# A gated linear-scan mixer with a routed expert: new written-out orders per batch, four staging slots, planes added in pairs before their transposes

## The reference

```python
x = L0_attn_x                                    # (8, 1024, 256) float32
z = layernorm(x)
logits = z @ gate_W                              # 4 mixers, the best 2 are kept, softmax over the 2
g, v, d = (z @ W[m] + b[m] for W in (Wg, Wv, Wd))  # for each mixer m of 4
a = 0.001 + 0.998 * sigmoid(d)
h_t = a_t * h_(t-1) + sigmoid(g_t) * tanh(v_t)   # a scan over the 1024 tokens, per mixer
x = x + layernorm(sum over m of comb[m] * h[m])
u = layernorm(layernorm(x)) ...                  # then per batch: mean over tokens -> batchnorm -> router
e = argmax(softmax(...)); y = relu(u @ W_down[e] + b) @ W_up[e] + b
x = x + layernorm(y * gate)
```

## Time and profile before

| | us |
|---|---|
| median of 3 runs | 859.58 |
| the profiled execution | 857.58 |
| its span | 855.8 |
| batch 0, up to its T0 | 99.8 |
| batches 1 to 6, each (619.9 / 6) | 103.3 |
| batch 7 from T0, and the end | 136.1 |

### The profile page before, as it was taken

How to read it: one execution, slowest core, us unless ns; L and a number is a source line. 1 busy time by engine, 2 the same in 40 slices (tenths; PEclk the granted TensorE clock), 3 DMA queues, 4 the chain that set the end, 5 groups by cost and what they waited for, 6 DMA issues and landing times. The chain is left out here.

```text
span 855.8 us, 11078 instructions
## 1 busy us (share of the span) xinstructions
PE 686.4 (80%) x3577; PEld 364.6 (43%) x3577; DVE 601.7 (70%) x1233; ACT 464.1 (54%) x803; POOL 74.8 (9%) x57
## 2 busy tenths in 40 slices
PE   4989795798948898689987889687895878998823
PEld 2454443345423463344634336243453435543521
DVE  6878766675854949459494686846768467778886
ACT  4756254655555544755457564565645745585522
POOL 1010011001110103001030010200111001000110
PEclk9989997899978999689997999988997899999965
DMA  9700230004300061000510007000160002300003
GB/s 220 250 26 1 86 112 1 10 1 133 115 0 11 0 199 52 0 10 1 198 50 1 10 4 243 4 0 10 33 215 2 9 1 75 123 1 9 2 0 107
DMA packets 40624, 49.78 MB, mean 58 GB/s; under 512 B 6470, under 2 KB 36458, under 8 KB 40554
## 3 DMA queue, kind: packets, MB, share of 16 engines
q1 hardware_dynamic: 33164, 41.62, 15.5%
q10 hardware_dynamic: 7392, 7.34, 3.0%
HBM read 38.85 MB, written 8.52 MB: 55 GB/s over the span
## 5 line engine op out<-in xcount | busy, mean ns | idle before, releaser
L1135 PE MATMUL ps_main<-xh,w_hi 128*128 128x512 f16 x768 | 301.8, 393 | 6.5 <-ACT decay_s L494 3.9
L1135 PE MATMUL ps_main<-xh,w_lo 128*128 128x512 f16 x768 | 300.3, 391 | 0.0
L1135 PE MATMUL ps_main<-xl,w_hi 128*128 128x512 f16 x768 | 298.8, 389 | 0.0
L761 DVE TENSOR_TENSOR_SCAN hid<-decay_s,value_s 128x1024 f32<-128x1024 f32 (+1 forms) x64 | 138.1, 2158 | 6.1 <-DVE value_s L779 0.6
L494 ACT ACTIVATE gate_s<-ps_main,vecs 128x512 f32<-128x512 f32 x128 | 87.6, 685 | 99.0 <-PE ps_main L1135 92.5
L494 ACT ACTIVATE value_s<-ps_main,vecs 128x512 f32<-128x512 f32 x128 | 88.1, 689 | 94.1 <-PE ps_main L1135 92.8
L494 ACT ACTIVATE decay_s<-ps_main,vecs 128x512 f32<-128x512 f32 x128 | 88.4, 691 | 84.8 <-PE ps_main L1135 81.2
L1135 PEld LDWEIGHTS ps_main<-xh,w_hi 128*128 128x128 f16 x768 | 77.9, 101 | 98.6 <-issue 10.1
L1135 PEld LDWEIGHTS ps_main<-xl,w_hi 128*128 128x128 f16 x768 | 77.1, 100 | 97.3 <-issue 11.7
L1135 PEld LDWEIGHTS ps_main<-xh,w_lo 128*128 128x128 f16 x768 | 77.2, 100 | 87.4 <-issue 9.1
L779 DVE TENSOR_TENSOR value_s<-gate_s,value_s 128x1024 f32<-128x1024 f32 (+1 forms) x72 | 79.4, 1103 | 41.8 <-ACT value_s L494 41.6
(11 more groups left out here) (138 smaller groups left out, 587.8 us busy)
## 6 DMA issues: line engine op xcount, KB each, us to landing
comb_all<-comb_dram SPq DMA_DIRECT2D x32, 512.0 KB, 5.1
resid<-in_L_attn_x SPq DMA_DIRECT2D x8, 1024.0 KB, 5.5
x_in<-in_L_attn_x ACTq DMA_DIRECT2D x14, 512.0 KB, 7.0
out<-resid SPq DMA_DIRECT2D x7, 1024.0 KB, 8.6
expert<-experts SPq DMA_DIRECT2D x8, 192.5 KB, 2.2
x_in<-in_L_attn_x SPq DMA_DIRECT2D x2, 512.0 KB, 4.8
w_stage<-in_L_attn_Wg SPq DMA_DIRECT2D x4, 256.0 KB, 5.6
w_stage<-in_L_attn_Wd SPq DMA_DIRECT2D x4, 256.0 KB, 7.0
```

Of the source, the lines that this page charges most:

```text
L761: dve.tensor_tensor_scan(states(pc), staged(decay_s, pc, pc.c), staged(value_s, pc, pc.c), start, ALU.mult, ALU.add).then_inc(scanned, 1)
L1135: ins = pe.matmul(ps_main[:, i % BANKS], w[:, 3 * m + kind, k, half * P:(half + 1) * P], v[:, bt.par, k, chunk(c)], start=(n == 0), stop=( ...
```

## The change

- `run` is split: `run_first`, `run` and `last` each have an order of their own on every engine.
- Gates and decays have four slots (`SLOTS`), and the value of a piece goes straight to its place in `hid`; `value_s` is gone. `multiply` and `scan` work in place there. The new waits are on ScalarE, before a value is written over a plane of the batch before.
- Planes 2, 3, 6 and 7 (`SUMMED`) are weighted, and then the plane two places before (same half, the mixer before) is added on VectorE. Only these four are transposed: 32 transposes in a batch instead of 64.
- x is held once instead of twice. Its load is issued by SyncE, at the start of `run`, behind the store of the batch before; it was issued by ScalarE.
- VectorE's order: `a_moments` and `residual` stand together ahead of piece 0, `t_moments`, `scale_t` and `x_moments` together ahead of piece 1; before, `x_moments` was the first, and pieces stood between the others.
- The ranking of the mixers has 9 instructions instead of 15. Places `i` of nearly all other work change.

```diff
+SUMMED = (2, 3, 6, 7)
-        x_in = sb("x_in", [P, 2, T, D])
+        x_in = sb("x_in", [P, T, D])
-        gate_s = sb("gate_s", [P, 2, S])
-        value_s = sb("value_s", [P, 2, S])
-        decay_s = sb("decay_s", [P, 2, S])
+        gate_s = sb("gate_s", [P, SLOTS, S])
+        decay_s = sb("decay_s", [P, SLOTS, S])
...
             # SyncE
+            def load_next_x(bt, nx):
+                sp.wait_ge(x_normed, done(bt))
+                for c in range(C):
+                    load_x_chunk(nx, c)
+            def run(bt, nx, pv):
+                load_next_x(bt, nx)
+                load_resid(bt)
+                load_expert(pv)
+                load_weights(bt, nx)
+                store(pv)
...
             # ScalarE, evacuate
-                behind = 3 if bt.cut and pc.q >= 2 else 1
+                behind = 2 * SLOTS - 1 if bt.cut and pc.q >= SLOTS else SLOTS - 1
+                if kind == VALUE and fresh and not first and (pc.c or 0) == 0:
+                    if pc.plane in SUMMED:
+                        act.wait_ge(plane_turned, len(SUMMED) * (bt.n - 1) + SUMMED.index(pc.plane) + 1)
+                    else:
+                        act.wait_ge(weighed, PLANES * (bt.n - 1) + pc.plane + 3)
             # ScalarE, run_first
+                    if i == 0:
+                        mixer_high(1)
+                    if i == 4:
+                        shares(bt)
+                        mixer_high(2)
+                    if i == 7:
+                        mixer_high(3)
...
+                    if i == 46:
+                        shares(nx)
             # ScalarE, run
-                        if i in (17, 18):
-                            normalise_t(pv, tiles(i - 17))
+                    if i == 16:
+                        normalise_t(pv, tiles(0))
+                    if i == 19:
+                        normalise_t(pv, tiles(1))
...
-                    if i == 38:
+                    if i == 44:
                         shares(nx)
+                    if i == 45:
+                        act.wait_ge(y_scaled, pv.n + 1)
+                        scale_rows(pv, (0, 1, 2), normed)
+                    if i == 46:
+                        scale_rows(pv, (3, 4, 5), normed)
+                    if i == 47:
+                        scale_rows(pv, (6, 7), normed)
...
             # VectorE
             def weigh(bt, pc):
...
-                dve.tensor_tensor(src, src, comb_all[:, m, tokens(pc.c)], ALU.mult).then_inc(weighed, 1)
+                if pc.plane not in SUMMED:
+                    dve.tensor_tensor(src, src, comb_all[:, m, tokens(pc.c)], ALU.mult).then_inc(weighed, 1)
+                    return
+                dve.tensor_tensor(src, src, comb_all[:, m, tokens(pc.c)], ALU.mult).then_inc(second_weighed, 1)
+                dve.wait_ge(second_weighed, len(SUMMED) * (bt.n + (pc.c or 0)) + SUMMED.index(pc.plane) + 1)
+                dve.wait_ge(weighed, PLANES * bt.n + pc.q - 1)
+                dve.tensor_tensor(src, hid[:, pc.plane - KT, tokens(pc.c)], src, ALU.add).then_inc(weighed, 1)
...
             # TensorE, run
+                    if i == 2:
+                        turn_planes(pv, (2, 3, 6, 7))
+                    if i == 22:
+                        turn_u(pv)
+                    if i == 25:
+                        route(pv)
+                    if i == 31:
+                        down(pv)
+                    if i == 32:
+                        pe.wait_ge(h_ready, done(pv))
+                        turn_x(nx)
+                    if i == 39:
+                        pe.wait_ge(xl_ready, KT * C * (nx.n + 1))
+                        up(pv)
+                    if i == 40:
+                        gates(nx)
+                    if i == 45:
+                        turn_weights(nx)
```

More of the change, by code:

```diff
@@ L42 @@
 BANKS = 3
+SLOTS = 4
 CHUNK = 512
@@ L446, in last @@
                 power("y", y_root_in, y_root, pv)
[L447 to L454, removed]
+                power("a", a_root_in, a_root, bt, 0)
+                power("t", t_root_in, t_root, bt, 0)
+                power("a", a_root_in, a_root, bt, 1)
+                power("t", t_root_in, t_root, bt, 1)
+                power("y", y_root_in, y_root, bt, 0)
+                power("y", y_root_in, y_root, bt, 1)
+            iterations(pool, run_first, run, last)
         @block.scalar
@@ L630, in _ @@
+            iterations(act, run_first, run, last)
         @block.vector
@@ L1003, in run @@
[L1003 to L1019 removed]
+                a_moments(pv)
@@ L1020, in run @@
+                y_moments(pv)
+                rank_mixers(nx)
+                scale_y(pv)
                 weights_of(nx)
-                piece(bt, pcs[6], pv is None, between=(lambda: scale_y(pv)) if pv else None)
+                multiply(bt, pcs[6])
+                scan(bt, pcs[6])
                 copy_weights(nx, False)
-                if not pv:
-                    prepare_hidden_biases(prep)
-                piece(bt, pcs[7], pv is None)
-                if pv:
-                    finish(pv)
+                weigh(bt, pcs[6])
@@ L1029, in last @@
+                multiply(bt, pcs[7])
+                scan(bt, pcs[7])
+                weigh(bt, pcs[7])
+                finish(pv)
             def last(bt, pv):
@@ L1081, in last @@
-                for c in range(C):
-                    finish_late(bt, c)
-            iterations(dve, run, last)
+                low_u(bt, 1)
+                join_h(bt, 0)
+                low_h(bt, 0)
+                join_h(bt, 1)
+                low_h(bt, 1)
+                y_moments(bt, 0)
+                y_moments(bt, 1)
+                scale_y(bt, 0)
+                finish_late(bt, 0)
+                scale_y(bt, 1)
+                finish_late(bt, 1)
+            iterations(dve, run_first, run, last)
@@ L1239, in run, with last @@
+                    product(bt, i, bank, False)
+            def last(bt, pv):
+                for i, bank in enumerate(banks(bt)):
+                    if i == 1:
+                        turn_planes(pv, (2, 3, 6, 7))
+                    if i == 15:
+                        turn_u(pv)
+                    if i == 19:
+                        route(pv)
+                    if i == 25:
                         down(pv)
                     if i == 31:
-                        gates(nx)
-                    if i == 36 and pv:
@@ L1243, in run @@
                         up(pv)
[L1244 to L1260 removed]
+                    if i == 37:
@@ L1269, in last @@
                 down(bt)
-                for c in range(C):
-                    up(bt, c)
-            iterations(pe, run, last)
+                up(bt, 0)
+                up(bt, 1)
+            iterations(pe, run_first, run, last)
 _INS = ["L0_attn_x", "L0_attn_Wg", "L0_attn_bg", "L0_attn_Wv", "L0_attn_bv", "L0_attn_Wd", "L0_attn_bd",
```

569 lines of the change are left out of this document (313 added, 256 removed).

## The result

The changed kernel takes 748.65 us (median of 4 runs, 747.77 to 749.35). The kernel before, measured beside it, takes 860.12 (858.15 to 860.99). The ratio is 0.8706, 95% interval 0.8688 to 0.8725: 111 us less. The profiled execution took 748.79, its span 747.0. Forecast were 766, range 737 to 812, and faster at 0.94.

What follows compares the result with a forecast made beforehand. A late load of x delays a, residual, t and u, bounding a batch's first half; TensorE bounds the second. 93.5 + 2.6 + 528 (six batches of 88) + 139 = 763 of span, 765 with what surrounds it; forecast 766, range 737 to 812.

Steps and rivals of the forecast that it cites:

- two waits for roots: Steady batch, VectorE: GpSimd's roots of a and t are uncovered, a stall of 2.2 us each, 4.4 in all.
- a wait for plane 7: Start of a steady batch: TensorE waits 2 to 3 us for VectorE's last piece, which is ready at +8.2.
- the walk: One steady batch followed through each engine's new order from the end of product 47: next one at +86.9, period 85.8.
- I stacked: Load of x issued at about +11 behind the store, 7.0 and 8.6 us one behind the other: lands at +27.
- Batch 0: First batch: ends at 93.5 instead of 99.8 us; bounds 9 less and 2 more.
- The carry of 2.6: Batch 0 into batch 1: VectorE is 2.6 us later there than in a steady batch.
- the 2.2 us a batch: Steady batches: added to the period of 85.8 for joints and low clock after waits, bounds 0 and 6.
- my terms up to the shift of t: Steady batch: 10.5 + 3.65 + 2.2 + 3.2 + 4.8 + 3.65 + 2.2, written as +31.
- Batch 7 with its end: Last batch, VectorE the bound: 139 us instead of 136.1; bounds 4 less, 6 more.
- B: Steady batches: waits for plane 7 and the share move on, half the gain kept, 95 to 96 each, 811; 0.20 including late x.
- D: TensorE's clock: 1.2 GHz after each wait and low through the second half, kernel slower at 900 us; chance 0.05.
- C: Steady batches: TensorE and VectorE overlap better, VectorE's 75 busy plus two roots, 80 each, 718 in all; chance 0.06.

Runs made afterwards that it cites:

- run 3: Changed kernel with the statistics of x put first again in VectorE's steady order, GpSimd's root of x first too; 837.29 us, ratio 0.975.
- Run 12: Changed kernel without pairs, with mixer_low, ranking and weights_of ahead of the experts' preparation on VectorE in batch 0; 720.29 us, ratio 0.84.
- run 5: Changed kernel without the adds in pairs: all eight planes transposed and accumulated in PSUM, 64 transposes a batch; 723.19 us, ratio 0.8427.
- run 4: Changed kernel with two slots of gates and decays instead of four; 752.28 us, ratio 0.8771.
- run 1: Kernel before with the statistics of x moved behind piece 1 on VectorE, GpSimd's root of x behind that of t; 831.96 us, ratio 0.9697.
- run 8: Changed kernel with piece 0 between a's statistics and the residual, and x's statistics between those of t and scale_t; 767.68 us, ratio 0.8907.
- run 6: Changed kernel with the four adds of a batch left out and the 32 transposes kept, output incomplete; 721.74 us, ratio 0.8408.

## Why the prediction was right, and where not

**The mechanism held.** Nearly all that it named as signs came: the 7.33 us at the statistics of x are gone, those of a start at +10.05 (said +10.5), two waits for roots (1.81 and 1.88; said 2.2), rows of t at +29.5 (said +31.6), a wait for plane 7 of 2.17 (said 2 to 3), route at +45.0 (said +47.5) with a wait of 2.69 (said 2.9), and from route to the next T0 39.2 us (the walk had 39.4). ScalarE stood for VectorE at no gate and no value in that batch. One sign failed narrowly: batches were to be 85 to 92 us apart, and are 84.7. And x lands sooner than I stacked it: run 3, where VectorE waits for it and its load is issued at the same place, has it at +20.1, not at +27. As the prediction says, the sum is the same by either.

**The sum, term by term.** Batch 0 ended at 96.0, not 93.5. VectorE stood 6.09 us for the experts' loads with the ranking queued behind it, and TensorE 4.27 for it:

```profile
24.19 0.17 DVE L993 TENSOR_SCALAR small<-vecs 128x2 f32<-128x2 f32 x1 [6.09 <-DMA resid<-in_L_ffn_b_up]
```
```profile
31.26 0.40 PE L1250 MATMUL ps_misc<-ident,comb 128*32 128x128 f32 x1 [4.27 <-DVE comb L799]
```

I had priced the gates' wait for this preparation at 2.3, but not the ranking behind it. Run 12 took this stall away and gained about 1 us, so the remainder of the 2.5 stays open. The carry of 2.6 held: batch 1 took 87.2, the five others 84.7. So six batches were 6 x 84.7 where I had 6 x 88, 19.8 too many. **This is the term that was mis-sized**: the 2.2 us a batch that I added to my walk (85.8) for joints and low clock. In the followed batch low clock costs 1.7 us, beside VectorE's chain, with 2.69 us of waiting at route behind it, and so nothing. The other 1.1 lies in the first half, where route comes 2.5 us early in the followed batch. Of these 0.5 are the earlier start of a's statistics, and 0.8 are an error in adding: my terms up to the shift of t make 30.2, not the 31 that I wrote. The two roots are 0.7, since they let VectorE wait 1.81 and 1.88 instead of the 2.2 that I took. Batch 7 with its end came to 140.3 against 139; VectorE's pieces ended at +98.9 (said +98.4). Together 2.5 - 0.1 - 19.8 + 1.3 = -16.1: 763.1 forecast, 747.0 measured. That batches 0 and 7 took 3.8 us more than forecast hides a part of the miss in the steady batches, which is luck. The bare walk gives 93.5 + 2.6 + 6 x 85.8 + 139 = 750.

**The rivals.** B (811) and D (900) didn't come, since waits are short and the clock 0.98. C's number (718) is not the changed kernel's. It is near run 5 (723.19), but a batch takes 82.0 there and not the 80 of C, and VectorE has no adds, so C's reason isn't what that run shows.

**What the sum did not see.** It priced the adds at 4.9 us of VectorE and the transposes at 3.7 of TensorE, and both disappeared in a walk of 88. It never asked what the walk would be without them. Run 5 answers: 2.7 a batch less and 7 at the end (and 2.4 in batch 0). And I wrote that four slots pay for the two uncovered roots; run 4 shows that two slots do as well in every steady batch.

**Where the 111 us come from.** Moving x alone gives 26 to 28, VectorE's new order (with x moved) 33, all that is new except the place of x 23 (run 3). Together they give 111, more than twice the sum of 28 and 23. By the traces each part alone leaves the same chain a, residual, t, u waiting elsewhere: for transposes that stand too late on TensorE (run 1), or for a load (run 3). The pairs take back 25 of what would be 137. How the remainder divides over the single new places on TensorE and ScalarE was not tried.

## What to carry to other kernels

With in-order queues, follow the chain that crosses the engines and put nothing before its links that isn't part of it: a load at the head of VectorE's queue cost 4.6 us a batch in one order (a wait of 7.33) and 14 in the other (10.0), so the price of a stall is that of the order around it, and not its length alone. Here, moving one engine's work without the places of the others' gave a third of the gain. Before work is moved from one engine to another (adds for transposes), walk the batch without the move as well; 3.7 us a batch saved on TensorE were worth at most about 1.5 in the whole kernel, since they had covered a wait, and 4.9 us a batch on a VectorE busy for 75 of 84 cost 27. And an idle gap on a busy engine isn't filled for nothing unless the work for it is ready and fits into the gap.

## What the runs showed of the chip

GpSimd's root of 8 columns depends on what VectorE does. GpSimd in the followed batch:

```profile
281.65 1.64 POOL L439 TENSOR_TENSOR root_a<-root_in_a,neg_half 128x8 f32<-128x8 f32 x1 [19.28 <-DVE root_in_a L731]
295.23 1.64 POOL L439 TENSOR_TENSOR root_t<-root_in_t,neg_half 128x8 f32<-128x8 f32 x1 [11.95 <-DVE root_in_t L731]
300.94 2.52 POOL L439 TENSOR_TENSOR root_x<-root_in_x,neg_half 128x8 f32<-128x8 f32 x1 [4.08 <-DVE root_in_x L731]
```

It takes 1.64 us while VectorE waits for it and 2.52 beside a piece; it was 2.54 beside one before. Beside the statistics of x, which read one input, it takes 1.64 as well; this is run 8:

```profile
299.19 1.64 POOL L439 TENSOR_TENSOR root_t<-root_in_t,neg_half 128x8 f32<-128x8 f32 x1 [11.54 <-DVE root_in_t L731]
```

The Trainium skill, "GPSIMD Engine Reference", "Specifications", says that GpSimd's SBUF interfaces are shared with VectorE and contended by its instructions with two SBUF inputs, which these pieces are; the trace agrees.

TensorE ran low behind the wait of 2.17 us in the followed batch (8 matmuls), behind 4.27 in batch 0 and 14.66 in run 3, but not behind the 2.69 at route nor behind the 1.54 at x's transposes. At route itself, a wait of 1.75 us was followed by low matmuls in run 6 (1.2 us behind it, 7 of them) and by none in run 5. So the length of one wait doesn't tell by itself whether the clock falls, and these runs don't settle what else does.
